# Edge sums of two graph layers as dense products of a count matrix, made during the relation attention

## What is computed

```python
x = x + L0_gnn(ln(x), edges, edge_type_64, ...);  x = x + L0_ffn(ln(x), ...)   # edge attention; 2 of 8 experts
x = x + L1_gnn(ln(x), edges, edge_type_6, ...);   x = x + L1_ffn(ln(x), ...)   # attention over 6 relations; 2 of 8
# L2: a plain edge sum
h = deg_isqrt * (ln(x) @ W2.T + b2);   x = x + deg_isqrt * segment_sum(h[src], dst);   x = x + L2_ffn(ln(x), ...)
# L3: an edge sum with a loop at each node
h = dinv * (ln(x) @ W3)
x = x + leaky_relu(dinv * (segment_sum(h[src], dst) + h) + b3, 0.2);   x = x + L3_ffn(ln(x), ...)
```

## Time and profile before

| | us |
|---|---|
| median of 3 runs | 5675.99 (5674.44 to 5685.74) |
| span of the profiled execution | 5709.5 |
| PE busy in it | 4142.4 (73%) |
| DVE busy | 2438.6 (43%) |
| POOL busy | 2168.6 (38%) |
| ACT busy | 1163.7 (20%) |
| DMA, moved | 639.34 MB, mean 112 GB/s |

### The profile page before, as it was taken

The page is one execution under the profiler, slowest core; times in us unless marked ns, Lnnn a source line. Parts: engine busy times, 40 slices in busy tenths (PEclk is TensorE's granted clock), DMA queues, the critical chain, the costliest instruction groups (busy, mean ns, idle before and its releaser), DMA issues. The chain is left out here.

```text
span 5709.5 us, 67954 instructions
## 1 busy us (share of the span) xinstructions
PE 4142.4 (73%) x19769; PEld 3142.0 (55%) x19769; DVE 2438.6 (43%) x4746; ACT 1163.7 (20%) x2671; POOL 2168.6 (38%) x2090
## 2 busy tenths in 40 slices
PE   5788884654816666799976999455559999555668
PEld 2555553443614444599975888333437677334445
DVE  4577778877234444356655000421223222212244
ACT  1233330001220000232322444100004333000023
POOL 0566654554436666000000210466650000566621
PEclk9888887996958888899986999677779999777789
DMA  2677874530743223210012998233330000233310
GB/s 77 208 243 241 250 215 151 162 98 23 235 128 88 85 86 86 86 38 8 7 41 82 336 323 281 89 88 93 87 97 26 1 1 16 75 91 88 91 37 23
DMA packets 375879, 639.34 MB, mean 112 GB/s; under 512 B 73053, under 2 KB 270072, under 8 KB 375424
## 3 DMA queue, kind: packets, MB, share of 16 engines
q1 hardware_dynamic: 275262, 342.97, 18.4%
q0 software_dynamic: 100288, 292.14, 17.6%
HBM read 526.37 MB, written 108.57 MB: 111 GB/s over the span
## 5 line engine op out<-in xcount | busy, mean ns | idle before, releaser
L2554 PE MATMUL sum_ps<-gathered_rows,hit 128*125 (+1 forms) x3328 | 1061.5, 477 | 842.0 <-issue 561.2
L2468 POOL DMA_INDIRECT gathered_rows<-k_table,index x1176 | 1160.8, 987 | 1281.1 <-ACT index L2457 717.6
L2554 PEld LDWEIGHTS sum_ps<-gathered_rows,hit 128*125 128x125 f32 (+1 forms) x3328 | 744.9, 235 | 1158.0 <-issue 1033.1
L97 POOL DMA_INDIRECT rows_all<-kv_table,src_of_visit x416 | 448.5, 1078 | 310.6 <-issue 135.5
L2538 DVE TENSOR_TENSOR node_sums<-node_sums,sum_ps 125x256 f32 x244 | 102.3, 419 | 918.0 <-DMA composed<-in_L_gnn_b 495.7
L2457 ACT ACTIVATE index<-src_of_chunk 128x4 int32<-128x4 int32 x294 | 59.2, 205 | 1647.0 <-DMA gathered_rows<-k_table,index 1581.1
L777 PE MATMUL ps_q<-q,hit_t 125*128 x832 | 322.5, 473 | 5.9 <-issue 5.2
L1057 PE MATMUL ps_sum<-summand,hit 128*125 128x261 f32 x832 | 211.6, 397 | 147.1 <-DVE odd_sums L1017 123.2
L2538 DVE TENSOR_TENSOR window_sums<-window_sums,sum_ps 126x256 f32 x344 | 144.8, 421 | 348.2 <-PE sum_ps L2554 183.0
L2762 PE MATMUL qk_ps<-window_sums,composed 128*128 128x126 f32 (+1 forms) x2400 | 292.1, 279 | 0.0
L1996 DVE TENSOR_TENSOR y<-out_ps,b 128x256 f32<-128x256 f32 x120 | 50.9, 424 | 551.2 <-PE out_ps L1895 464.0
(11 more groups left out here) (478 smaller groups left out, 6714.6 us busy)
## 6 DMA issues: line engine op xcount, KB each, us to landing
w<-in_L_ffn_W SPq DMA_DIRECT2D x112, 1024.0 KB
v_kept<-rows_all SPq DMA_DIRECT2D x104, 512.0 KB
v_rows<-v_kept SPq DMA_DIRECT2D x104, 512.0 KB, 3.6
gathered_rows<-k_table,index POOLq DMA_INDIRECT x1176
w<-in_L_ffn_w SPq DMA_DIRECT2D x64, 256.0 KB
b<-in_L_ffn_b SPq DMA_DIRECT2D x88, 128.0 KB
y_slots<-y SPq DMA_DIRECT2D x32, 256.0 KB
y_slots<-y SPq DMA_DIRECT2D x56, 128.0 KB
```

The source lines that it names most:

```text
L97: pool.indirect_dma_start(env.ring[:, k % KEPT_RING, i, :], None, env.kv_table, bass.IndirectOffsetOnAxis(env.src_of_visit[:, k * VB + i:k ...
L2468: pool.indirect_dma_start(self.rows[:, (q % SLOTS) * CHUNKS + c, :], None, self.table, bass.IndirectOffsetOnAxis(self.index[:, q % SLOTS, ...
L2554: mm = pe.matmul(sum_ps[0:rows, k % banks, 0:D], hit[:, g % (lead + 1), i * chunks + c, :], gather.rows[:, ds(first[i] + c, 1), :].rearran ...
```

## The change

A count matrix is made once, beside the relation attention, and used twice.

- Setup makes a third table of another kind: 704 visits (`AV`) of an edge chunk and a window of ten destination nodes (313 windows, `AN`), with two keys per edge: the source's place within its tile of 125, and 10 x (source's tile) + (place within the window). They are kept in HBM as bf16. The quad table goes.
- In the relation attention, DVE turns the keys of four visits at a time into two 0/1 matrices in bf16 (`make_hits`). PE multiplies them, one product of 125 x 250 to a visit, into one PSUM bank that is never cleared, so that it holds the counts of all edges so far (`count`). ACT copies the bank to SBUF after each visit (`copy_count`), PE's next count waits for that copy. SP stores the copies of two visits at a time to `counts` in HBM (`store_seen`), from a ring of four. The hooks stand between the old instructions, 30 in a full group. DVE's adds of `mix` move to POOL. Eleven groups of windows stay in SBUF instead of 17, so 83 windows are spilled and brought back instead of 47.
- `node_sum_phase` replaces `gather_sum_phase` for L2 and L3. SP and ACT fetch, for each window, the copy made at its last visit (even windows SP, odd ones ACT, into 50 slots). DVE subtracts each from the next, which gives the window's counts, already laid out as the left operand. PE does 25 x 25 f32 products of 125 x 125 with 125 x 256, whose right operand is the table of rows, kept in SBUF (`env.table`). DVE finishes a tile at once: L2's update, or L3's loop, scale, bias and bend, with POOL's add to x.
- The tables are no longer stored to `k_table` by `routed_experts_phase` "L1" and `wide_tail_phase`, and both tails lose their updates.

```diff
+AW = 10
+AN = -(-N // AW)
+AC = T * AW
+AV = QUADS * CHUNKS + AN - 1
+AB = 4
+AS = 2
...
+def node_sum_phase(env, kind):
...
+        def fetch(engine, k, which):
+            if k >= marks:
+                engine.wait_ge(taken, k - marks + 2)
+            for w in windows_in(k):
+                if w % 2 == which:
+                    row = engine.value_load(env.last_visit[0:1, w:w + 1], min_val=0, max_val=AV - 1)
+                    engine.dma_start(seen[:, w % WINDOW_SLOTS, :], env.counts[:, ds(row, 1), :].rearrange(
+                        "p o c -> p (o c)")).then_inc(landed[k % marks], 16)
...
+                    v.tensor_tensor(out(first, n), here(slot + first, slot + n), here(slot + first - 1, slot + n - 1),
+                                    ALU.subtract).then_inc(taken, 1)
...
+                for i in range(T):
+                    b, half = divmod(i, 2)
+                    pe.wait_ge(taken, pieces_before(i))
+                    if i >= banks:
+                        pe.wait_ge(added, i - banks + 1)
+                    for t in range(T):
+                        mm = pe.matmul(sum_ps[0:P, i % banks, 0:D], count[:, b % 2, t, half * P:(half + 1) * P], env.table[:, t, :],
+                                       start=t == 0, stop=t == T - 1)
+                    mm.then_inc(summed, 1)
...
-KEPT = 17
+KEPT = 11
+HIT_RING = 6
+SEEN_RING = 4
+STORE_LAG = 8
...
+                def store_seen(b):
+                    sp.wait_ge(copied, (b + 1) * AS)
+                    sp.dma_start(env.counts[:, b * AS:(b + 1) * AS, :], seen[0:P, b % SEEN_RING]).then_inc(seen_stored[b % SEEN_RING], 16)
...
                     if g < NS - KEPT:
                         bring_back(g)
+                    upto = min(AV, visits_before(g + 1) + STORE_LAG) // AS
+                    for b in range(gone, upto):
+                        store_seen(b)
+                    gone = upto
                     sp.wait_ge(o_made, g + 1)
...
+                def count():
...
+                    pe.wait_ge(hits_made, 2 * (n // AB + 1))
+                    if n > 0:
+                        pe.wait_ge(copied, n)
+                    at = n // AB % HIT_RING
+                    pe.matmul(count_ps, row_hit[:, at, 0:P, n % AB], key_hit[:, at, :, n % AB], start=n == 0,
+                              stop=True, skip_group_check=True).then_inc(counted, 1)
...
+                            if counting and (i, c) == (1, 0):
+                                count()
                     mm.then_inc(projected, 1)
+                    if counting:
+                        count()
...
+                def copy_count():
...
+                    if n % AS == 0 and b >= SEEN_RING:
+                        act.wait_ge(seen_stored[b % SEEN_RING], 16 * (b // SEEN_RING))
+                    act.wait_ge(counted, n + 1)
+                    act.activation(seen[0:P, b % SEEN_RING, n % AS, :], count_ps, ACT.Copy).then_inc(copied, 1)
...
+                        for which, hit, n in ((1, row_hit, 128), (0, key_hit, AC)):
+                            v.tensor_tensor(hit[:, b % HIT_RING], ranks[:, 0:n, :],
+                                            cell_key[:, which, b * AB:(b + 1) * AB].unsqueeze(1).to_broadcast([128, n, AB]),
+                                            ALU.is_equal).then_inc(hits_made, 1)
...
-            gather_sum_phase(env, env.k_table, env.src_of_chunk, env.quads, env.node_sums, P, 1)
-            wide_tail_phase(env)
-            gather_sum_phase(env, env.k_table, env.src_of_chunk, env.quads, env.node_sums, P, 1, False)
-            small_tail_phase(env)
+        node_sum_phase(env, "L2")
+        wide_tail_phase(env)
+        node_sum_phase(env, "L3")
+        small_tail_phase(env)
```

More of the change, by code:

```diff
@@ L204, in setup_phase @@
         sel = [sb(env, st, f"sel{j}", [QUADS, n, v]) for j, (n, _, _, v, _) in enumerate(passes)]
-        behind = {1: sb(env, st, "behind1", [QUADS, 1]), 2: sb(env, st, "behind2", [QUADS, 2])}
-        quad_key = sb(env, st, "quad_key", [128, env.quads.visits, CHUNKS])
+        behind = sb(env, st, "behind", [QUADS, 2])
+        cell = {n: sb(env, st, f"cell_{n}", [128, AV]) for n in ("dst", "inside", "src", "tile")}
+        cell_key = sb(env, st, "cell_key", [128, 2, AV], BF16)
         rel_w = sb(env, st, "rel_w", [128, env.pairs.visits, 2])
@@ L310, in _ @@
                     ins.then_inc(selected, 1)
-                    tiles = env.tile_of_visit if out is None else out.tile
-                    done(v.tensor_copy(tiles[0:1, 0:visits], tile_bc[j][0:1, :]))
+                    if j < 2:
+                        tiles = env.tile_of_visit if out is None else out.tile
+                        done(v.tensor_copy(tiles[0:1, 0:visits], tile_bc[j][0:1, :]))
                     if out is not None:
@@ L334, in _ @@
                                                 in1=rel_w[:, :, c], op0=ALU.mult, op1=ALU.add))
+                v.sem_inc(window_read, 1)
                 done(v.scalar_tensor_tensor(out=in_a[:], in0=in_a[:], scalar=1.0, in1=in_b[:], op0=ALU.add, op1=ALU.mult))
                 done(v.tensor_scalar(env.pairs.key[:], in_a[:], -1.0, None, ALU.add))
+                v.wait_ge(cell_values, 1)
+                halves = ((4, 0, 512), (5, 512, AV))
+                for b, lo, hi in halves:
+                    done(v.scalar_tensor_tensor(out=cell["dst"][:, lo:hi], in0=tile_bc[2][:, lo:hi], scalar=float(-AW),
+                                                in1=bank[b][:, 0:hi - lo], op0=ALU.mult, op1=ALU.add))
+                    done(v.tensor_copy(cell["src"][:, lo:hi], bank[b + 2][:, 0:hi - lo]))
@@ new lines, in _ @@
+                done(v.tensor_scalar(cell["inside"][:], cell["dst"][:], 0.0, None, ALU.is_ge))
+                done(v.scalar_tensor_tensor(out=cell["inside"][:], in0=cell["dst"][:], scalar=float(AW), in1=cell["inside"][:],
+                                            op0=ALU.is_lt, op1=ALU.mult))
+                done(v.tensor_scalar(cell["tile"][:], cell["src"][:], 1.0 / P, -0.496, ALU.mult, ALU.add))
+                done(v.tensor_scalar(cell["tile"][:], cell["tile"][:], float(3 * 2 ** 22), None, ALU.add))
@@ new lines, in _ @@
+                done(v.tensor_scalar(cell["tile"][:], cell["tile"][:], float(-3 * 2 ** 22), None, ALU.add))
+                v.scalar_tensor_tensor(out=cell_key[:, 1, :], in0=cell["tile"][:], scalar=float(-P), in1=cell["src"][:],
+                                       op0=ALU.mult, op1=ALU.add).then_inc(cells_made, 1)
+                done(v.scalar_tensor_tensor(out=cell["dst"][:], in0=cell["tile"][:], scalar=float(AW), in1=cell["dst"][:],
+                                            op0=ALU.mult, op1=ALU.add))
@@ L337, in _ @@
+                done(v.scalar_tensor_tensor(out=cell["dst"][:], in0=cell["dst"][:], scalar=1.0, in1=cell["inside"][:],
+                                            op0=ALU.add, op1=ALU.mult))
+                v.tensor_scalar(cell_key[:, 0, :], cell["dst"][:], -1.0, None, ALU.add).then_inc(cells_made, 1)
                 v.wait_ge(turned, 1)
                 done(v.tensor_copy(env.src_of_chunk[:].rearrange("p q c -> p c q"),
-                                   bank[4][:, 0:CHUNKS * QUADS].rearrange("p (c q) -> p c q", c=CHUNKS)))
@@ L345, in _ @@
+                done(v.tensor_copy(env.pairs.need[:], bank[2][0:1, 0:2 * QUADS].rearrange("p (u q) -> p q u", u=2)))
+                done(v.tensor_copy(env.pairs.slot[:], bank[3][0:1, 0:env.pairs.visits]))
+                done(v.memset(env.last_visit[:, AN - 1:AN], AV - 1))
+                done(v.tensor_scalar(env.last_visit[:, 0:AN - 1], bank[0][0:1, 1:AN], -1.0, None, ALU.add))
             @block.tensor
@@ L2192, in measure @@
                     for t in group(g):
-                        update(t)
-                    for t in group(g):
-                        v.wait_ge(updated, t + 1)
                         moment(t, 0)
@@ L3123, in _ @@
                 v.wait_ge(prepared, 3)
-                for t in range(GT):
-                    update(t)
                 done(v.tensor_scalar(rank[:], env.iota[0:P, 0:ne], -1.0, float(ne), ALU.mult, ALU.add))
@@ L3129, in _ @@
                 normalise(0)
-                for t in range(GT, 2 * GT):
-                    update(t)
                 choose(0)
@@ L3299, in routing_buffers @@
     env.gates = sb(env, st, "gates", [P, T, 8])
-    rows_all = sb(env, st, "rows_all", [128, 2 * KEPT_RING * VB if ring else T, D])
-    env.rows = rows_all[0:P, 0:T, :]
-    if ring:
+    if not ring:
+        env.rows = env.table[:]
+    else:
+        rows_all = sb(env, st, "rows_all", [128, 2 * KEPT_RING * VB, D])
+        env.rows = rows_all[0:P, 0:T, :]
         env.ring = rows_all[:].rearrange("p (s v two) d -> p s v (two d)", v=VB, two=2)
```

387 lines of the change are left out of this document (258 added, 129 removed).

## The result

The changed kernel takes **5542.2 us** (median of 4 runs, 5539.3 to 5547.2), and the kernel before, on the same chip, 5680.9 (5674.4 to 5692.7): ratio 0.975, 95% interval 0.9733 to 0.9767. The forecast was 5611, range 5400 to 5790. So it is faster by 139 us where I said 65: the direction and the range hold, the size is more than twice the one forecast. The profiled execution has a span of 5537.7 us, against 5709.5 before.

The account below looks back on a forecast made before the run. It took POOL's row gathers to bound the old node sums and PE the attention, with five-engine transfers setting all three stages after: +14 +218 -278 -19 = -65 us, 5644.5 times 0.994, 5611 us, range 5400 to 5790.

Parts of the forecast that it names:

- I take the middle, 93: Node sums: count-table fetches run at 93 GB/s, between 99 and 86 for the load of x; 420 us a phase.
- Setup, +14: Setup: a third visit table of 704 columns replaces one of 122, adding net 14 us, all on the path.
- Compose, nothing: Compose: spilling 83 windows instead of 47 costs nothing, 13 us at most if its cover were gone.
- So the stores decide: Attention: count stores on five DMA engines take 760 us, more than PE and ACT need; stage 800 us, +218.
- PE and ACT need 646 us: Attention: 23.5 groups at 27.5 us each for the 704 visits, a count priced at 0.12 us.
- The bound from above, 0.45: Attention: a count at the f32 price of 0.45 us makes a group 39 us, 930 in all, +350.
- the fetch decides: Node sums: fetching 39.1 MB takes 420 us, above the product's 282 to 381; 443 us a phase, -278 for both.
- The ends: Phase ends: no k table stores (-12), L2's updates (-2), L3's update and bend (-5); -19 in all.
- The missing cap: Rival, all stages: new transfers are not held to five engines; attention PE-bound, node sums 307 us, 5227 scaled; chance 0.10.
- Rows of 1000 and 2000 bytes: Rival, count stores and fetches: they move worse than 1 and 2 KB rows, fetches 86 GB/s; 5730 scaled; chance 0.22.
- The count chain with a falling clock: Rival, attention: PE waits for ACT's copy at each count, clock falls to 0.74; +444, 5836 scaled; chance 0.21.
- Attention over 865 us refutes the sign: Sign for the attention stage: if it took over 865 us, the forecast that the kernel gets faster would be refuted.

Follow-up runs that it names:

- fast_narrow: one_by_one with 125 rows stored and fetched again instead of 128, products keeping 128 weight columns: 5580 us, ratio 0.9766.
- half_bytes: Changed kernel with counts kept and fetched as bfloat16, still 125 rows: 5364 us, ratio 0.9433.
- unit_stride: wide_both with hits laid out visit by visit, so TensorE reads neighbouring elements of both operands: 5284 us, ratio 0.9289.
- one_by_one: unit_stride's layout on wide_both, each visit's hits made by two VectorE comparisons with a per-partition scalar: 5267 us, ratio 0.9271.
- wide_both: Changed kernel with 128 count-matrix rows instead of 125 in stores and fetches, the last three zero: 5326 us, ratio 0.938.
- aligned_rows: Changed kernel with the count table's rows 1024 bytes apart instead of 1000, stores becoming two packets of 1000 bytes: 5574 us, ratio 0.9767.
- adds_on_vector: Changed kernel with the six adds of a group moved back from GpSimd to VectorE: 5561 us, ratio 0.9742.
- one_queue: Changed kernel with all fetches of both node sums issued from SyncE's queue instead of two in turn: 5696 us, ratio 0.9974.

## Why the prediction was right, and where it was wrong

The direction was right, and so was what limits each of the three stages: transfers on five engines. The size was wrong, 139 us for 65, and the step that failed is the rate of the fetches, "I take the middle, 93", worth some 160 us; the rate of the stores failed too, the other way, by 76.

**Setup, +14**: +14.6. The cell products took 9.6 us for the 11.7 worked out. **Compose, nothing**: it takes 49 us in both.

**"So the stores decide"** in the attention: right, shown by fast_narrow. **Its price was too low**, 760 us for the counting where 820 were measured. The step that failed is "88.0 MB at 128 GB/s is 688 us": the 128 was the kv table's store, of 2 KB rows in a stretch of 2 us, and stores alone make 110 here, which is 800 us. The 72 us added for shared traffic and gaps were too many, 22 would have done. Together +61; 23 more are the stretches before the first visit and behind the last, 29 and 33 us where I had 24 and 15, and the old stage was 588, not 582.

**"PE and ACT need 646 us"**: also too low, 799 by half_bytes. The count was priced at 0.12 us, "half a record". That price is right for neighbouring operands and 128 weight columns (0.11 to 0.13 in unit_stride); this kernel's has 125 columns and a stride of four elements, and takes 0.27 to 0.29 between the projections and 0.20 between the values. Looking up the operands' layout in the diff, where a hit tile is indexed with n % AB in its last place, would have shown the second. The bound from above, 0.45, held it. The way a group is added up failed too: where a count does cost 0.11 to 0.13, in unit_stride and one_by_one, the counting takes 708 and 701 us, not 646. And the upper end doesn't follow from its own rule: with 0.45 the same steps give some 35 us a group and 850 in all, not 39 and 930. The cheap copy was nearly right too (0.33 for 0.377). Since the stores are slower still, this error cost only the expectation of slack: the two limits lie 22 us apart, not 114.

**The node sums, "the fetch decides"**: right (284 us as soon as the fetches are quick). **"I take the middle, 93"** is the step that failed: the fetches run at 115 GB/s in mid-phase, and the phase takes 363 us in place of 443. The rows it came from, the load of x, moved 86 and 99 GB/s at the same share of 0.34; why 1 KB rows went slower there than 1000-byte rows here is not shown. That one queue gives 96 doesn't explain it: there the pace of SyncE's issues is the limit, at a share of 0.31, while the load of x is one DMA of 3125 KB, so the likeness of 93 and 96 is chance. The prediction says that each queue owes one DMA per 2.7 us and doesn't ask what one engine can issue; with two it was enough. In the profiled spans the change is 107 us larger than forecast: 159 from the node sums, 10 from the ends and 15 from the pair gather that the change doesn't touch, less the attention's 76. **The product at 282**: PE is busy 272 us in wide_both, in a phase of 284 where 307 was said.

**The ends**, -19: -29, the router's 7 included.

**The rivals.** The missing cap: refuted, with the signature that was named (0.32 to 0.36 in all three stages, 0.52 with 128 rows). Rows of 1000 and 2000 bytes: starts off a boundary are refuted as its mechanism by aligned_rows, for the side in HBM; of its prices, the fetches' 86 GB/s is wrong, while the stores came out even slower than its 120. The count chain with a falling clock: the clock stayed at 0.99, though the stage did pass the 865 us that were named for it. "Attention over 865 us refutes the sign" was wrong as a sentence: the stage took 882 us, and the sign held, because the node sums gave more. A threshold on one stage holds only with the others as forecast.

**GpSimd's adds**, costed at nothing: nothing (adds_on_vector).

## What to carry to other kernels

A tile that is a few rows short of 128 pays twice here: transfers of 125 rows went on five DMA engines of sixteen, and 125 bf16 weight columns load in 192 ns for 114. Filling up with three zero rows took the ratio from 0.975 to 0.938, and laying the operands out for TensorE's reads, not for VectorE's writes, took it to 0.929 and 0.927 (unit_stride, 5284 us, and one_by_one, 5267): either is the version to keep. Take a rate from a row with the same direction and the same packet, sustained. Divide a phase by its number of DMAs per issuing engine too: 313 fetches at 1.3 us are 410 us, whatever the DMA engines could move. And two limits that lie 22 us apart hide each other until one is taken away.

## What the hardware showed beyond what was expected

- Reading every fourth bf16 element made a 250-column product's record 382 ns for 267, and a 128-column weight load 114 for 95.
- SyncE started fetches of 125 rows at best once per 1.3 us, with 1000 bytes a row (one_queue) and with 500 (half_bytes). A second issuing engine raised fetches of 1000-byte rows on five DMA engines from 96 to 115 GB/s, and did nothing for stores that were due once per 2.3 us (822 and 828 us).
- Half the bytes in the same number of packets freed the fetches entirely: the phase fell from 363 to 287 us, its product's time, at a share of 0.26.
- GpSimd's add took a different time with other work of VectorE beside it: POOL's 138 operations took 117.6 us beside two-operand hits in wide_both (0.85 each), 151.9 beside the slower ones of unit_stride (1.10), 102.3 beside one_by_one's comparisons with a scalar (0.74).
- TensorE's granted clock, in L2's node sum: 0.98 with PE busy 272 of 285 us (wide_both), 0.91 with 293 of 363 (the kernel after), 0.85 with 303 of 428 (one_queue); the same 625 products (1250 records) took 272, 293 and 303 us of records.
